# Attention stage: low parts of projected rows behind the next unit's maxima, and the second turned bank copied by VectorE in two of eight units

## The reference, cut to what matters

```
x = x + attention(layernorm(x))

q, k, v = x @ Wq + bq, x @ Wk + bk, x @ Wv + bv        # 16 heads of 16 features
s = q @ k.T / sqrt(16) - slope[h] * (T - 1 - j)        # T = 256, per sequence and head
s = where(j <= i, s, lowest)
p = softmax(s)
out = (p @ v) @ Wo + bo
```

## Time and profile before

| | us |
|---|---|
| median of 3 runs | 1869.94 (1866.65 to 1870.73) |
| profiled execution | 1869.54 |
| its span in the trace | 1867.4 |
| attention stage in it | about 1540 to 1726 |
| TensorE busy, whole span | 1791.4 (96%) |
| VectorE busy | 1332.9 (71%) |
| ScalarE busy | 950.2 (51%) |
| GpSimd busy | 580.6 (31%) |

### The profile page before, as it was taken

The page is one execution under the profiler, slowest core; times in us unless marked ns, Lnnn a source line. Parts: engine busy times, 40 slices in busy tenths (PEclk is TensorE's granted clock), DMA queues, the critical chain, the costliest instruction groups (busy, mean ns, idle before and its releaser), DMA issues.

```text
span 1867.4 us, 26671 instructions
## 1 busy us (share of the span) xinstructions
PE 1791.4 (96%) x9573; PEld 1382.1 (74%) x9573; DVE 1332.9 (71%) x1870; ACT 950.2 (51%) x1807; POOL 580.6 (31%) x399
## 2 busy tenths in 40 slices
PE   7999999999799999998799999999999998999999
PEld 6888888888354545534578888888888886777888
DVE  6666666567999999999976666565676556777533
ACT  3542323333688768787645433233334327988422
POOL 1000143100388879888730000000000024655000
PEclk9999999999899999999999999999999999999999
DMA  5232335211122222223203233132121306663100
GB/s 200 83 96 74 99 119 164 63 62 35 52 75 71 75 79 74 71 68 117 81 18 81 73 97 104 63 107 63 63 71 56 65 1 125 114 128 74 38 12 23
DMA packets 84203, 146.41 MB, mean 78 GB/s; under 512 B 13864, under 2 KB 23720, under 8 KB 83560
## 3 DMA queue, kind: packets, MB, share of 16 engines
q1 hardware_dynamic: 84072, 144.72, 27.3%
HBM read 130.38 MB, written 14.29 MB: 77 GB/s over the span
## 4 chain that ended last, share of the span: by engine, by line
PE 78%; DVE 11%; issue 5%; ACT 4%; POOL 2%; DMA 0%; DVEq 0%; SPq 0%; POOLq 0%; ACTq 0%
PE psum L161 20%; PE psum L162 19%; PE psum L163 19%; PE psum L1521 6%; DVE scan_state L1722 5%; PE psum L1375 2%; PE psum L2124 2%; POOL scan_state L1249 1%; ACT attn_p L2272 1%; PE psum L1473 1%; PE psum L278 1%; DVE moe_hidden_lo L866 1%; PE psum L2078 1%; DVE X L822 1%; PE psum L2141 1%
## 5 line engine op out<-in xcount | busy, mean ns | idle before, releaser
L793 ACT ACTIVATE moe_hidden_hi<-moe_hidden 128x512 fp32r<-128x512 f32 x200 | 126.3, 631 | 399.2 <-DVE moe_hidden L846 398.3
L1249 POOL TENSOR_TENSOR scan_state<-scan_delta_u,scan_B_rows 128x1024 f32<-128x1024 f32 x127 | 299.3, 2367 | 80.5 <-PE psum L1521 59.5
L161 PE MATMUL psum<-xnT_hi,moe_w_hi 128*128 128x512 f32 x800 | 316.5, 396 | 2.6 <-DVE xnT_lo L475 2.3
L162 PE MATMUL psum<-xnT_lo,moe_w_hi 128*128 128x512 f32 x800 | 314.5, 393 | 0.0
L163 PE MATMUL psum<-xnT_hi,moe_w_lo 128*128 128x512 f32 x800 | 312.4, 390 | 0.0
L1722 DVE TENSOR_TENSOR_SCAN scan_state<-psum,scan_state 128x1024 f32<-128x1024 f32 x128 | 291.4, 2281 | 0.3
L842 DVE TENSOR_TENSOR moe_gated_up<-moe_gate_rows,psum 128x512 f32<-128x512 f32 x184 | 126.6, 688 | 210.1 <-PE psum L163 124.7
L423 POOL TENSOR_SCALAR rstd<-mean_var 128x2 f32<-128x2 f32 x48 | 10.6, 220 | 743.2 <-DVE mean_var L457 743.1
L161 PE MATMUL psum<-moe_w_hi,moe_hidden_hi 128*128 128x256 f32 x800 | 230.3, 288 | 3.6 <-DVE moe_hidden_lo L866 2.2
L1521 PE MATMUL psum<-scan_state,ident 128*128 128x512 f32 x480 | 228.4, 599 | 2.2 <-DVE scan_gated L1737 1.4
L163 PE MATMUL psum<-moe_w_hi,moe_hidden_lo 128*128 128x256 f32 x800 | 226.2, 283 | 0.0
(11 more groups left out here) (234 smaller groups left out, 3503.4 us busy)
## 6 DMA issues: line engine op xcount, KB each, us to landing
scan_B_rows<-scan_B SPq DMA_DIRECT2D x127, 256.0 KB, 3.1
moe_gate_rows<-gate_table SPq DMA_DIRECT2D x176, 128.0 KB, 3.0
moe_w_raw<-moe_pack SPq DMA_DIRECT2D x50, 384.0 KB, 4.1
attn_stack<-attn_rows SPq DMA_DIRECT2D x96, 128.0 KB, 5.8
moe_gate_rows<-gate_table SPq DMA_DIRECT2D x32, 224.0 KB, 3.2
ffn_w_raw<-ffn_pack SPq DMA_DIRECT2D x16, 384.0 KB, 4.4
moe_gate_rows<-gate_table SPq DMA_DIRECT2D x32, 160.0 KB, 2.6
moe_gate_rows<-gate_table SPq DMA_DIRECT2D x24, 192.0 KB, 2.9
```

The source lines that it names most:

```text
L161: e.matmul(out, wH, xH, start=start, stop=False)
L162: e.matmul(out, wH, xL, start=False, stop=False)
L793: e.activation(self.hH[:, b, :], self.hb[:, b, :], ACT.Copy).then_inc(self.s_hH.sem, 1)
L1249: e.tensor_tensor(self.st[q % self.NBUF][:], self.dtu[:, 2 * h:2 * h + 2, :], self.Bs[:, q % self.RING, :].unsqueeze(1).broadcast_to([P, 2 ...
```

## The change

Two edits. In units 0 and 4 of every chunk (`SECOND`) the second turned bank is copied to `pT` by VectorE, ahead of the third one, and no longer by ScalarE; since both copies count in the same semaphore, VectorE first waits until the first bank's copy of that unit has been counted. And the low parts of the q and k projections (`rows_lo` as slot 1 job of u1, u2, u4, u5) are no longer done by VectorE at the end of their own unit but in the next one, right behind its two maxima.

```diff
+    SECOND = (0, 4)
...
@@ scalar
             if n != self.N - 2:
                 keep(n, 0)
-                keep(n, 1)
+                if u not in self.SECOND:
+                    keep(n, 1)
...
@@ vector
         def keep(n):
+            if n % self.UNITS in self.SECOND:
+                e.wait_ge(self.s_T.sem, self.s_T.at(3 * n + 2))
+                if n > 1:
+                    e.wait_ge(self.s_pv.sem, self.s_pv.at(n - 1))
+                e.wait_ge(self.s_pt01.sem, self.s_pt01.at(2 * n + 1))
+                e.tensor_copy(self.pt[:, n % 2, 1, :], ps[:, 4, :]).then_inc(self.s_pt01.sem, 1)
             e.wait_ge(self.s_T.sem, self.s_T.at(3 * n + 3))
...
+        def rows_of(n):
+            it = self.job(*divmod(n, self.UNITS), 1)
+            return bool(it) and it[0][0] in "qk"
...
                 second(n + 2)
+            if n and rows_of(n - 1):
+                job(*divmod(n - 1, self.UNITS), 1)
             norm(c, u)
             job(c, u, 0)
             keep(n)
             if n and n % 2 == 0:
                 out_lo(n // 2 - 1)
-            job(c, u, 1)
+            if not rows_of(n):
+                job(c, u, 1)
```

## The result

| | before | after |
|---|---|---|
| median, us | 1870.34 (1866.65 to 1871.74, 6 runs) | 1885.55 (1882.19 to 1887.82, 6 runs) |
| ratio of times | | 1.0078 (1.0066 to 1.0090) |
| profiled execution, us | 1869.54 | 1885.49 |
| its span, us | 1867.4 | 1883.4 |
| TensorE busy, us | 1791.4 (96%) | 1798.5 (95%) |

The change costs 15.2 us by the medians and 14.6 by the ratio, 0.8%; the forecast was 13.3. Eight copies did change engines, as the busy times show, but they moved 3 to 4 us of busy time and the span grew by 16.0.

The account below looks back on a forecast made before the run. TensorE bounds the kernel, in a loop with VectorE's maxima and ScalarE's exponentials. Wait 11.0, early maxima -1.2, low-part delays 2.2 and clock 1.3 make +13.3 on 1869.54: 1882.8 us, range 1875.5 to 1889.

Parts of the forecast that it names:

- u0: chunks 1, 2, 3: VectorE's wait in u0 delays the next maxima and scores: +1.6, +1.6 and +1.9 us; chunk 0 hidden.
- u4 with the stack: chunks 0, 1, 2: Wait in u4, 1.4 us each, plus k1's late projection 0.3 (chunk 0) or late stack loads 1.0, 0.4 (chunks 1, 2).
- u4, chunk 3, at the end: The wait in chunk 3's u4 delays the first maximum, straight into the last units' chain: +1.6 us.
- early maxima in u3: Moved low parts let u3's maxima start earlier, so u4's scores come sooner in chunks 0 to 2: -1.2 us.
- projections' wait in u2, u6: TensorE's next projection into bank 7 waits for the later low part: +0.1 at six places, +0.5 us with rounding.
- clock: One more fall of TensorE's clock, after the idle stretch in u1 of chunk 3: +1.3 us.
- Part 1: In u0 and u4 VectorE's second-bank copy waits for ScalarE's first, delaying maxima and scores: +11.0 us, bounds 7.5 and 13.3.
- Part 2: Low parts behind the maxima: -1.2 us gained in u3, +2.2 us from later projections and stack loads.
- its used-up old wait: Chunk 1: TensorE already waited for stack loads before the change, so later loads add +1.0 us at u6's scores.
- Part 3: Of seven new idle stretches of TensorE, one, u1 of chunk 3, halves the clock: +1.3 us; bounds none or +8.
- VectorE comes late anyway: Rival: VectorE reaches its copy after ScalarE's first, so Part 1 is nothing and only the stack is late: 1872.4 us, chance 0.05.
- The clock rival: TensorE's clock falls at nearly every new gap: +20 us, 1889.4 us, chance 0.06.

Follow-up runs that it names:

- e5: Kernel before, with VectorE in u0 and u4 only waiting for ScalarE's first-bank copy, no copy or low part moved: 1884.28 us, ratio 1.0070.
- e4: Kernel before, with the second banks of u0 and u4 copied by VectorE without the order wait, low parts unmoved: 1871.19 us, ratio 1.0001.
- e6: Kernel after, but in unit 28 (u4 of the last chunk) ScalarE makes both copies: 1883.98 us, ratio 1.0070.
- e8: Kernel after, plus six unread TensorE products in each of u1 and u5 of the last chunk: 1883.88 us, ratio 1.0064.
- e2: Kernel before, with only the q and k low parts moved behind the next unit's maxima: 1876.61 us, ratio 1.0028.
- e7: Kernel before, with the low parts of q0, q1 and k1 moved behind the maxima, k0's left in place: 1870.63 us, ratio 1.0002.
- e9: Kernel before, plus six unread TensorE products in u3 of chunk 0: 1870.13 us, ratio 0.9992.
- e10: Kernel before, plus six unread TensorE products in each of u0 and u3 of chunk 0: 1869.84 us, ratio 0.9991.
- e1: Kernel after, with the low parts put back at the end of their own unit: 1890.02 us, ratio 1.0102.
- e11: Kernel before, plus unread products, six each in u0 and u3 of chunk 0, four each in u1 and u4 of chunk 3: 1867.77 us, ratio 0.9992.
- e3: Kernel after, but VectorE's second-bank copy neither waits for nor counts in the shared semaphore: 1877.21 us, ratio 1.0032.

## Why the prediction was right, step by step

Worked out of the two traces, in us; the whole is 201.84 - 185.95 = 15.9.

| step | forecast | measured |
|---|---|---|
| u0: chunks 1, 2, 3 | 1.6, 1.6, 1.9 | 1.7, 1.7, 2.0 |
| u4 with the stack: chunks 0, 1, 2 | 1.4 + 0.3, 1.4 + 1.0, 1.4 + 0.4 | 1.8, 2.3, 1.9 |
| u4, chunk 3, at the end | 1.6 | 1.8 |
| early maxima in u3 | -1.2 | -1.3 |
| projections' wait in u2, u6 | +0.5 | +0.6 |
| clock | +1.3 | +3.0 to +3.2 |
| beginning of the stage | none | +0.6 |

**Part 1 (the wait).** Right in mechanism, place and size. VectorE's idle time of 2.72 and 2.81 us, released by ScalarE's copy, is what was to be seen, and e5 shows that the wait alone does it, e4 that the copy without it costs nothing. Each microsecond of the earlier trace rows could be carried forward because the loop first maximum to next scores kept its 4.05 us. The hand-over from ScalarE's copy was 0.14 us instead of the assumed 0.04, which accounts for the 0.1 by which the places in u0 are over.

**Part 2 (low parts).** Right. The load issue that stood at 1662.65 is the row below of SyncE after, 9.4 us later where the chunk began 5.8 us later: 3.6 us late, as forecast. Chunk 1's u5 is the dearest place of all, 8.11, as its used-up old wait said; but that it came out so near the forecast is partly luck. e6 and e8 are the same kernel up to there and took 7.41 and 8.01 us in it, and 7.40 and 7.75 in chunk 2's u5 (7.49 here): the stack's share is known to some 0.7 us a place. e2 and e7 show the stack as its own cost; in the full change it is mostly hidden in part 1's.

```profile
1672.08 6.74 SPq L1959 DMA_DIRECT2D attn_stack<-attn_rows  x12
```

**Part 3 (clock), the term that was mis-sized.** "The longest is u1 of chunk 3 ... I take one more fall, there: +1.3". A fall came there and cost 0.7; that the change brings it is not shown, because e9 and e10, which leave chunk 3 as before, have it too (5.78 and 5.77). The dear one came where I had charged only the delay, "straight into the last units' chain": in u6 TensorE had nothing to do but wait 3.10 us for the third bank's copy, and the last units then ran at half clock, 2.3 us (from L278 to the next layer 10.20 against 7.89) to 2.5 (against e8's 7.73). In both kernels with a wait of 3.1 us there (after and e1) the clock fell; in those that waited 1.5 to 1.6 us at full clock (e2, e6, e8, e10, e11) it stayed up. I had listed the new idle stretches before the scores and never asked which later instruction waits for what queues behind the late maxima: x_stage and the third bank's copy. Two of the three old falls, one ahead of chunk 0's units (longer now) and one in u4 of chunk 0, were there before and stayed; a further one, behind u1 of chunk 0, belongs to the beginning, below. All this is one execution. An estimate for all of them: the ratio's 14.6 us less the 12.5 of the table's other steps leave some 2 us for the clock and the beginning together. The ratio's interval is 2 us wide to either side, so the term was too small by 1.7 to 1.9 us in the profiled execution, and by how much on average stays open. The Trainium skill (TensorE: Matmul & The Clock Gate, "Loop structure matters more than you think") shows the clock dropping over a long wait for a DMA while a PSUM copy by VectorE leaves it up; in its case the next products follow the copy at once. Here TensorE waited 3.10 us for just such a copy, with no product beside it, and the clock fell: what the page says of the copy does not carry over to a wait for it.

**The beginning.** u0 to u2 of chunk 0 are 0.6 us longer in the profiled execution after (31.50 against 30.88 us from the first scores to those of u3). e4, e7 and e9 need 31.5 too and show no change in their ratios, so this belongs to the one profiled execution of before and not to the change. What differs is again the clock: before was at full clock behind u1 of chunk 0, after and e1 to e9 were at half (rows in the last section), and e10 and e11, with TensorE kept busy in u0, were at full clock and needed 30.0 and 30.2.

**The rivals.** That VectorE comes late anyway is out by the wait's 21.9 us. The clock rival was the nearest: e5 has four dear falls worth 5.4 us, the change itself two worth 3.0 to 3.2 in the profiled execution. It was not far off: with the low parts at their old place (e1) the total was 1890.

## What to carry to other kernels

When two engines count in one semaphore, the order of the counts becomes a wait; look where the other engine stands in its own list, and price what queues behind the waiting instruction, not the instruction (here 13.4 us for a wait, nothing for the copy). A count of its own, or a count that comes later on the same engine anyway, avoids it. A delay in the last units of a stage can have a second price: where TensorE had no product beside the wait the clock fell, and six unread products beside it (e8) kept it up. And one trace tells where the clock fell in one execution only; before a fall is put down to a change, look whether it stands in kernels without it.

## What the runs showed of the hardware

The length of an idle stretch does not say by itself whether the clock falls. TensorE of the kernel before in u1 of chunk 0, idle 1.32 us and then at full clock (twelve transposes in 1.47 us):

```profile
1557.80 0.32 PE L2078 MATMUL psum<-attn_stack,attn_stack 50*128 50x128 f32 x1 [1.32 <-ACT attn_p L2272]
...
1559.00 1.47 PE L2124 MATMUL psum<-ident,attn_p 128*128 128x128 f32 x12
```

TensorE of the kernel after in the same unit, idle 1.33 us and then at half clock (twelve in 2.61):

```profile
1559.25 0.32 PE L2079 MATMUL psum<-attn_stack,attn_stack 50*128 50x128 f32 x1 [1.33 <-ACT attn_p L2273]
...
1560.46 2.61 PE L2125 MATMUL psum<-ident,attn_p 128*128 128x128 f32 x12
```

Why the one and not the other stays open. A fall costs nothing where TensorE isn't the one waited for: the kernel before had twelve transposes at half clock after its last scores, and reached L278 after 5.04 us; e6 did the same work at full clock and reached it after 5.04 us too. Elsewhere a fall cost 0.7 to 1.6 us, and 0.9 (e1) to 2.5 at the end. With products that nobody reads in the idle stretch the clock stayed up behind units 0, 3, 25, 28 and 29. Only behind unit 3 do all profiled kernels without them show half clock; behind the others some do and some don't (unit 25: after, e9 and e10 do, before, e3, e4 and e7 don't).
